# Two-layer recurrent kernel: the second layer's silu made by ScalarE itself, four units in a row, instead of from tanh and a product

## The reference

```python
x = silu(causal_conv4(xn @ W_in_x) + conv_b)      # 256 channels = 2 tiles of 128
dt, B, C = split(x_proj(x)); delta = softplus(dt_proj(dt) + dt_b)
s_t = s_(t-1) * exp(delta * A_n) + (delta * x) * B_n    # 16 states n per channel
y = (sum_n s * C_n + x * Dskip) * silu(xn @ W_in_z);  s_out = y @ W_out
h_e = silu(xn @ Wg_e) * (xn @ Wu_e)                # 8 experts, 512 hidden each
f = sum_e cw_e * (h_e @ Wd_e)                      # every expert, weighted
```

## Time and profile before

| | |
|---|---|
| median of 3 runs | 913.11 us (912.3 to 918.16) |
| the profiled execution's own time | 914.93 us |
| its span, first to last instruction | 913.1 us |
| PE busy | 805.6 us (88%) |
| DVE busy | 682.9 us (75%) |
| POOL busy | 490.3 us (54%) |
| ACT busy | 420.7 us (46%) |
| mean granted TensorE clock | 0.971 |

### The profile page before, as it was taken

The page is one execution under the profiler, slowest core; times in us unless marked ns, Lnnn a source line. Parts: engine busy times, 40 slices in busy tenths (PEclk is TensorE's granted clock), DMA queues, the critical chain, the costliest instruction groups (busy, mean ns, idle before and its releaser), DMA issues.

```text
span 913.1 us, 10705 instructions
## 1 busy us (share of the span) xinstructions
PE 805.6 (88%) x2312; PEld 383.6 (42%) x2312; DVE 682.9 (75%) x1096; ACT 420.7 (46%) x699; POOL 490.3 (54%) x388
## 2 busy tenths in 40 slices
PE   2858998999899988868998987999887999889997
PEld 1324444444444443333454343544343544344443
DVE  4389359927973845349879897789896889899995
ACT  2744554455455634555334633434542434563341
POOL 0086436634660553225756656656655656757773
PEclk9979999999999989998999999999998999999999
DMA  9265255332523553167744575756565745758771
GB/s 266 57 189 136 89 169 150 104 106 83 161 54 106 150 169 88 31 162 193 186 146 125 131 186 143 187 128 154 143 154 131 178 132 141 176 138 212 189 186 35
DMA packets 85851, 129.28 MB, mean 142 GB/s; under 512 B 7368, under 2 KB 28560, under 8 KB 85808
## 3 DMA queue, kind: packets, MB, share of 16 engines
q1 hardware_dynamic: 85808, 128.85, 53.7%
HBM read 125.35 MB, written 3.47 MB: 141 GB/s over the span
## 4 chain that ended last, share of the span: by engine, by line
PE 30%; DVE 16%; issue 11%; ACT 4%; DMA 3%; POOL 1%; DVEq 1%; SPq 1%; ACTq 0%; POOLq 0%
DVE state L619 6%; PE bank L1496 6%; PE bank L1504 5%; DVE bank L612 3%; PE bank L1359 3%; PE bank L1397 3%; DMA CB<-crow 3%; PE bank L1384 2%; PE bank L1386 2%; PE bank L1444 2%; PE bank L1385 2%; DVE gg L739 2%; PE bank L1314 1%; DVE hid L747 1%; ACT sg L1225 1%
## 5 line engine op out<-in xcount | busy, mean ns | idle before, releaser
L619 DVE TENSOR_TENSOR_SCAN state<-decay,bank 128x512 f32<-128x512 f32 x192 | 232.9, 1213 | 17.5 <-issue 9.1
L1384 PE MATMUL bank<-XH,wh 128*128 128x512 f32 x256 | 176.3, 689 | 25.5 <-DVE gg L739 11.1
L1496 PE MATMUL bank<-xw,wu 128*128 128x512 f32 x256 | 141.9, 637 | 36.5 <-DVE hid L747 36.2
L1179 ACT ACTIVATE decay<-delta,negA 128x510 f32<-128x510 f32 x192 | 135.7, 715 | 42.0 <-DVE state L619 41.7
L1186 ACT ACTIVATE hid<-bank,early 128x512 f32<-128x512 f32 x128 | 87.5, 685 | 142.0 <-PE bank L1444 132.2
L612 DVE TENSOR_TENSOR bank<-bank,CB 128x512 f32<-128x512 f32 x192 | 133.2, 694 | 20.6 <-DMA CB<-crow 11.5
L1444 PE MATMUL bank<-hid,wd 128*128 128x512 f32 x256 | 147.5, 659 | 0.0
L902 POOL TENSOR_TENSOR product<-state,CB 128x512 f32<-128x512 f32 x64 | 81.7, 1276 | 99.9 <-DVE state L619 99.9
L1504 PE MATMUL bank<-hid,wd 128*128 128x512 f32 x256 | 132.4, 600 | 0.0
L1225 ACT ACTIVATE sg<-bank 128x512 f32<-128x512 f32 x128 | 75.7, 592 | 99.9 <-PE bank L1386 99.9
L898 POOL TENSOR_TENSOR product<-state,CB 128x512 f32<-128x512 f32 x64 | 81.6, 1276 | 74.4 <-DVE state L619 44.4
(11 more groups left out here) (167 smaller groups left out, 922.6 us busy)
## 6 DMA issues: line engine op xcount, KB each, us to landing
CB<-crow SPq DMA_DIRECT2D x256, 256.0 KB, 5.0
CB<-crow SPq DMA_DIRECT2D x64, 512.0 KB, 4.8
cwb<-cwrow SPq DMA_DIRECT2D x32, 256.0 KB, 5.7
wu<-W_dram SPq DMA_DIRECT2D x8, 256.0 KB, 5.3
wd<-W_dram SPq DMA_DIRECT2D x8, 256.0 KB, 5.9
wu<-Wu_dram SPq DMA_DIRECT2D x8, 256.0 KB, 3.6
xw<-Wg_dram SPq DMA_DIRECT2D x8, 256.0 KB, 4.6
wd<-Wd_dram SPq DMA_DIRECT2D x8, 256.0 KB, 5.0
```

The costliest lines, as they stand in the source:

```text
L619: v.tensor_tensor_scan(state[:, c % RING, :], decay[:, c % RING, :], drive, 0.0, ALU.mult, ALU.add).then_inc(state_ready.sem, 1)
L1179: a.activation(by_batch(decay[:, c % RING, :])[:, :, 1:], by_batch(delta[:, m, :])[:, :, 1:], ACT.Exp, scale=negA[:, c:c + 1]).then_inc(de ...
L1384: t.matmul(dst, wh[:, e, ws], XH[:, :], start=True, stop=False)
L1496: t.matmul(bank[UP_BANK][:, :], wu[:, e, 128 * f:128 * f + 128], xw[:, e % 2, :], start=True, stop=True).then_inc(up_ps.sem, 1)
```

## The change

Silu becomes one activation of ACT, for the experts' gates, for `xs` and for `sz`. What DVE did for it (L739, L701, L712) is gone, and so is `half_gate`. ACT now takes four units in a row in every fourth slot, then the decays of four or five chunks. The silu results and the decays get six places each (`PLACE`) in place of two and four. PE makes four gates in two slots, and none in the other two. The head's steps get other slots; `hand_over1`, `low1`, `form_delta` and the first two decays move from slot 0 into slots 29 to 31 of the pair before. In layer 1 only buffers and one wait (`sp_c_ready` for `sp_u_ready`) differ.

```diff
-HEAD1 = {6: "stat1", 7: "var1", 9: "xn", 11: "xnT", 12: "xi0", 13: "logits", 14: "lmax", 15: "lexp",
-         16: "xs0 z0 tz0", 17: "sz0 xi1", 19: "xs1", 20: "row0", 21: "z1 tz1 soft1", 22: "sz1",
-         24: "dt0 soft2", 25: "row1 rest0 soft3", 26: "dt1 less0", 27: "cwT rest1", 28: "less1 ln", 29: "xr"}
+HEAD1 = {6: "stat1", 7: "var1", 9: "xn", 11: "xnT", 12: "logits", 13: "lmax", 14: "xi0 lexp",
+         16: "xs0 z0 sz0", 17: "row0", 18: "xi1 soft1", 20: "xs1 z1 sz1", 21: "row1 soft2", 22: "dt0 soft3",
+         23: "rest0", 25: "dt1 less0 rest1", 26: "cwT less1", 29: "ln hand xr", 30: "low del0", 31: "dec0"}
...
+SCAN1 = [at + 1 for at in CHUNKS1]
+DECAYS1 = [[c for c in range(2, C1) if FT * e + 3 <= SCAN1[c] <= FT * e + 6] for e in range(E)]
+PLACE = [k % SIX for k in range(UNITS - FT)] + [0, 1, 4, 5]
...
+def freed(k, pair):
+    earlier = [n for n in range(k) if PLACE[n] == PLACE[k]]
+    if earlier:
+        return max(earlier) + 1
+    if isinstance(pair, int) and pair == 0:
+        return 0
+    return max(n for n in range(UNITS) if PLACE[n] == PLACE[k]) + 1 - UNITS
...
     # DVE
-            def finish_gate(i, u):
-                dve.wait_ge(tanh_ready.sem, tanh_ready.at1(i, u + 1))
-                dve.wait_ge(hid_ready.sem, hid_ready.at1(i, u - 1))
-                v.scalar_tensor_tensor(out=gg[:, u % 2, :], in0=sg[:, u % 2, :], scalar=1.0, in1=bank[HID_BANK + u % HIDS][:, :],
-                                       op0=ALU.add, op1=ALU.mult).then_inc(gg_ready.sem, 1)
...
-                v.tensor_tensor(hid[:, u % 2, :], gg[:, u % 2, :], bank[UP_BANK][:, :], ALU.mult).then_inc(hid_ready.sem, 1)
+                v.tensor_tensor(hid[:, u % 2, :], sg[:, PLACE[u], :], bank[UP_BANK][:, :], ALU.mult).then_inc(hid_ready.sem, 1)
...
     # ACT, head
+                if name in ("xs0", "xs1"):
+                    act.wait_ge(*use1(head_ps, j, f"xi{m}"))
+                    act.wait_ge(kept_ready.sem, kept_ready.at1(j, 0))
+                    act.wait_ge(dx_ready.sem, dx_ready.at1(j, 0 if m == 1 or first_pair(j) else -1))
+                    a.activation(xs[:, m, :], hb[:, :], ACT.Silu, bias=col1("bconv", m)).then_inc(head_read.sem, 1)
...
-                    a.activation(sz[:, m, :], hb[:, :], ACT.Tanh, scale=0.5).then_inc(tz_ready.sem, 1)
+                    a.activation(sz[:, m, :], hb[:, :], ACT.Silu).then_inc(head_read.sem, 1)
...
     # ACT, units
+            def silu(i, u):
+                act.wait_ge(hid_ps.sem, hid_ps.at1(i, u + 1))
+                act.wait_ge(hid_ready.sem, hid_ready.at1(i, freed(u, i)))
+                a.activation(sg[:, PLACE[u], :], bank[HID_BANK + u % HIDS][:, :], ACT.Silu).then_inc(silu_ready.sem, 1)
...
+                if u % FT == 0:
+                    silu(i, u)
+                    silu(i, u + 1)
+                    for name in steps_:
+                        if name in ("xs0", "xs1"):
+                            head(name, j)
+                    silu(i, u + 2)
+                    silu(i, u + 3)
+                    for name in steps_:
+                        if name in ("sz0", "sz1"):
+                            head(name, j)
+                    for c in DECAYS1[u // FT]:
+                        form_decay(i, c)
...
     # PE
-                pe.wait_ge(gg_ready.sem, gg_ready.at1(i, bank_free(u)))
+                pe.wait_ge(silu_ready.sem, silu_ready.at1(i, bank_free(u)))
...
-                if u == 0:
+                if u == 0 and first_pair(i):
                     gate1(i, 0)
-                if u + 1 < UNITS:
+                    gate1(i, 1)
+                if u % FT == 0:
+                    gate1(i, u + 2)
+                    gate1(i, u + 3)
+                if u % FT == FT - 1 and u + 1 < UNITS:
                     gate1(i, u + 1)
+                    gate1(i, u + 2)
+                if u == UNITS - 1 and head:
+                    gate1(j, 0)
+                    gate1(j, 1)
```

More of the change, by code:

```diff
@@ L319, in in1, with first_pair @@
             return lambda signal, n: signal.at1(i, n)
+        def first_pair(j):
+            return isinstance(j, int) and j == 0
         def over_e(ap):
@@ L728, in head1 @@
                     rounding(m, sp_u_ready.at1(j, m + 1))
+                if name == "low":
+                    if not first_pair(j):
+                        low1(j)
+                if name == "del0":
+                    form_delta(lambda signal, n: signal.at1(j, n), 0, J1, decay_ready.at1(j, 0 if first_pair(j) else -N))
             def low1(i):
@@ L760, in slot1 @@
                 at = in1(i)
-                if u == 0:
+                if u == 0 and late is first_late:
                     low1(i)
-                    if late is first_late:
-                        split_low(2 * E - 1)
+                    split_low(2 * E - 1)
                 if late:
@@ L773, in slot1 @@
                 if u == 0:
[L774 removed]
+                    form_dx(at, 0, 0, 0)
                     for c in now(CHUNKS1, u):
@@ L810, in _ @@
             v.memset(XNP[:, :, 0:KC - 1], 0.0).then_inc(setup_dve.sem, 1)
-            for k in range(RING):
+            for k in range(SIX):
                 v.memset(by_batch(decay[:, k, :])[:, :, 0:1], 0.0).then_inc(setup_dve.sem, 1)
@@ L1144, in head1 @@
                 if name == "ln":
-                    act.wait_ge(sp_u_ready.sem, sp_u_ready.at1(j, J1))
+                    act.wait_ge(sp_c_ready.sem, sp_c_ready.at1(j, J1))
                     a.activation(sp_l[:, :, :], sp_u[:, :, :], ACT.Ln).then_inc(sp_l_ready.sem, 1)
                     a.activation(warm[:, :], ones[:, :], ACT.Exp)
+                if name == "hand" and not first_pair(j):
+                    hand_over1(j)
+                if name == "dec0":
+                    for c in range(2):
+                        form_decay(j, c)
                 if name in ("dt0", "dt1"):
@@ L1219, in late0 @@
                     last.then_inc(tg_ready.sem, 1)
[L1221 removed]
+            def silu(i, u):
                 act.wait_ge(hid_ps.sem, hid_ps.at1(i, u + 1))
[L1224 to L1225 removed]
+                act.wait_ge(hid_ready.sem, hid_ready.at1(i, freed(u, i)))
+                a.activation(sg[:, PLACE[u], :], bank[HID_BANK + u % HIDS][:, :], ACT.Silu).then_inc(silu_ready.sem, 1)
             def slot1(i, u, head=None, j=None, late=None):
[L1228 removed]
+                if u == 0 and late is first_late:
                     hand_over1(i)
[L1230 to L1241 removed]
+                    split_high(2 * E - 1)
+                if u == 0 and late:
+                    late(u)
+                steps_ = now(HEAD1, u) if head else []
+                if u % FT == 0:
[7 more added lines that the diff above has]
+                    for name in steps_:
+                        if name in ("sz0", "sz1"):
+                            head(name, j)
+                    for c in DECAYS1[u // FT]:
+                        form_decay(i, c)
                 if u > 0 and late:
@@ L1245, in slot1 @@
                     keep(i)
-                if head:
-                    for name in now(HEAD1, u):
+                for name in steps_:
+                    if name not in ("xs0", "xs1", "sz0", "sz1"):
                         head(name, j)
```

91 lines of the change are left out of this document (29 added, 62 removed).

## The result

The changed kernel takes 940.97 us (938.98 to 946.61, 4 runs) against 914.62 (912.3 to 918.16, 4 runs) for the kernel before on the same chip: ratio 1.0286, 95% interval 1.0245 to 1.0327. It is slower by 2.9%, where 1.3% faster was predicted, and it lies outside the range. The profiled execution has a span of 938.9 us against 913.1, and a mean granted clock of 0.939 against 0.971.

The account below looks back on a forecast made before the run. DVE bounded plain slots, PE 0.05 us behind and next. Per pair, PE's 107.9 plus five terms (4.6, 5, 4.5, 3, 1.7) made 126.7 against 130.9; three pairs save 12.6, giving 901 us against 913.1, range 884 to 922.

Parts of the forecast that it names:

- the part on what is removed: DVE's work per full pair falls to about 89 us, below PE's 108; at most 23 us per pair gained.
- PE's floor: PE's unchanged work in a full pair of layer 2: 107.9 of 130.9 us at full clock.
- Term 1: At layer 2's loop jumps: PE idle and slower matmuls, 4.6 us per pair.
- Term 3: ACT in order: PE waits for silu behind head steps, 3.0 us at slot 11; 4.5 us per pair (0 to 9).
- Term 4: DMA queue: row1's send delays loads of CB for DVE's slot 24, 3 us per pair (0 to 4).
- Term 5: Waits of 3 us lower the clock: one stretch at the lower level, 1.7 us per pair (0 to 5).
- The range: Whole kernel: forecast's own 892 to 910 us, said to come from its terms' bounds; stated range 884 to 922.
- Layer 1's last pair: Carries the first head: four more switches, half shown in PE, 2.6 us, against 2.47 of waits for sz: nothing.
- The last pair: Layer 2, slots 6 to 31: four slots take 11.6 us on PE, 11.6 before on DVE: nothing gained.
- The drain: At ACT's table loads: the page adds about 1380 ns to 1283; the prediction saw none in the trace.
- The rivals: Whole kernel: waits hide, 873 (0.14); no switch, 889 (0.06); gain given back, 913 (0.25); slower, 927 (0.13).
- Rival E: PE waits for ACT's switch and silu at seven of eight gate groups, 13.3 us per pair: 927 us, chance 0.13.

Follow-up runs that it names:

- e1: The changed kernel with DVE's rest1 moved from slot 25 to 27 and POOL's less1 from 26 to 28: 916.65 us, ratio 1.0015 to the kernel before.
- e4: The kernel before with only rest1 moved from slot 27 to 26, beside dt1: 931.93 us, ratio 1.0168.
- e7: e5 with layer 2's three pairs written out in place of the loop on DVE, POOL, ACT and PE: 894.62 us, ratio 0.9751.
- e9: The kernel before with layer 2's three pairs written out, nothing else: 902.48 us, ratio 0.9858.
- e8: e5 with tanh in place of silu in layer 2, so no table switches there (the output differs): 903.36 us, ratio 0.9853.
- e6: e5 with a timetable of its own for the head in layer 1's last pair: 907.57 us, ratio 0.9904.
- e5: The changed kernel with rest1 in slot 27, less1 in 28 and xnT in slot 10: 912.01 us, ratio 0.9944 to the kernel before.
- e3: The changed kernel with tanh in place of silu in layer 2, so no table switches there (the output differs): 927.65 us, ratio 1.0118.
- e2: The changed kernel with the transposes of xn and ACT's copy of them in slot 10, not 11: 927.14 us, ratio 1.0131.

## Why the prediction was wrong

The sign was lost in the part on what is removed, at "DVE's work falls to about 89 us per pair, well below PE's 108, so PE is next, and this gain can't be taken whole". The 89 is right (88.6), the conclusion isn't. It treats DVE as a sum of busy times. An engine that runs in order also stands where it is told to stand, and the diff gave it a new place: rest1 in the slot of dt1. I went through ACT's order step by step and not through DVE's, because DVE was the engine being relieved. The prediction says of the step that is moved nothing at all. Undoing that one move takes the time from 940.97 to 916.65, 24 of the 26 us lost (e1), and making it in the old kernel costs 16 (e4). DVE stood 5.13 us for it where the sum of a pair has nothing.

By the prediction's own steps:
- PE's floor of 107.9: not refuted. The shortest pair of all runs is 120.6 (e7).
- Term 1, the jumps, 4.6 per pair: with the pairs written out, 4.5 in the old kernel (13.5 / 3) and 5.8 in the new (17.4 / 3). Good for the old; the second stop of DVE, 3.06, and PE's 7.33 for 5.45 are what was short.
- Term 3, ACT in order: at slot 11 the mechanism and the size of the wait were right, 2.73 against 3.0. Its price was not: 14 us for three pairs when taken away alone, 4.6 per pair, and 5 to 7 in all once rest1's wait was gone. All of PE's waits for a silu in layer 2 are 10.9 us, 3.6 per full pair where the term has 4.5.
- Term 4, the queue: 22.0 us of waits for CB in layer 2 against 6.8 before, 15.2 over four pairs, where I had 3 in each of three. The send, holds the queue as it did. Taking it out of the way gave 4.0 us in one kernel and none in the next, so most of these waits weren't on the path, or followed from others.
- Term 5, the lower clock: the mechanism was named and mis-sized. With the jumps and both misplaced steps gone PE is busy 336.0 us in the three pairs at 0.99 (e7), in the changed kernel 355.1 at 0.93 on the same work: 6.4 per pair, where terms 1 and 5 together have 1.6 + 1.7 = 3.3. In the old kernel the same difference is 2.7 per pair (348.8 against 340.6 in e9). I had waits of 3 us in mind; PE stands 4.05 for rest1 and 7.33 at the jump.
- The range: it was to come "from the bounds of its terms", and doesn't. With every term at its lowest a pair is 107.9 + 4.6 + 2 = 114.5, at its highest 107.9 + 4.6 + 8 + 9 + 4 + 5 = 138.5, which gives 864 to 936 us and not 892 to 910 (the stated range, 884 to 922, was then taken from the rivals' chances). The measured pair, 136.8, lies within those bounds; the measured time, 941, lies outside even them, by layer 1's last pair.
- Layer 1's last pair, "nothing": it lost 11.8. The switches of that head cost 5.3 there (e8), where I had set half of them against a saving of 2.47. PE waits 5.4 for the silu of xs at the two z, where the old kernel had only the 2.47 for DVE's sz; a timetable that parts them brings PE's first gate 4.8 earlier (e6). The two overlap, since without switches these waits are 2.6 us, so together they explain 5 to 10 of the 11.8, and the rest stays open. The delta product, which the change moved into DVE's slot 30, stands 5.52 us for the logarithm of ACT's slot 29, and the prediction never asks what slot 30 costs; but e6 shows that this wait cost nothing.
- The last pair, "nothing": it gained 2.8. The forecast compared plain slots, which are alike; the gain lies in the slots in which DVE had a further product (4.36 and 3.50 us before), and at the end.
- The drain that the Trainium skill, "ScalarE: Activation LUTs", section "What ACT_TABLE_LOAD costs", adds to a load: none in this trace either. The load began 0.02 us behind the copy (739.87 to 739.89), and the silu 0.01 behind the load (741.17 to 741.18). The prediction was right to go by the row.

The rivals did no better. Rival E, the slower side, came out nearest in time (927) with the wrong engine: ACT's switches hold PE for a few us, not 13 per pair (e8: 1.7 per full pair in e5's timetable, e3: 3.4 in the changed one). The chance of 0.12 for slower came from that mechanism only.

With both misplaced steps mended the pair is 127.5 where 126.7 was forecast. The near hit is luck in part, since slot 11's term is gone from it and others were low. And the time is only 0.6% below the old kernel's (e5), not 1.3%, because layer 1's last pair keeps its loss (XH at 410.5 for 398.9).

## What to carry to other kernels

When a change rewrites a hand-made timetable, go down each engine's column and ask of every step whether what it waits for was made in the same slot, and by how many engines: PE to ACT to DVE in one slot made DVE stand 5 us here; with DVE's step two slots later that wait was at most 1.6. Do this for the engine that gets relieved too, for its new idle time is only useful if nothing in its order blocks what PE needs next. And price a wait of PE with what follows it: here 2.7 us cost 4.6 to 5.8. Before blaming a long wait, ask what would have ended next: DVE's 5.5 us for the logarithm were replaced by as long a wait for something else.

## What the runs showed of the hardware

- DVE stopped at two instructions in a row after one jump of a loop, 3.74 and 3.06 us, waiting for nothing that the profile shows; writing four engines' loops out left 1.4 us of such stops (e7), and took 13.5 us (old kernel) and 17.4 us (new) from two jumps.
- After a PE wait of 2.73 us the granted clock went to its lower level within the next matmuls (passes 0.43 apart, not 0.23); after one of 4.05 us it was 0.57 from 664 to 668 us. Taking such a wait away shortened PE's busy time about as much as its idle time (e1: 9.8 and 10.3 us; e2: 8.3 and 9.0). With the jumps gone the clock in layer 2's three pairs was 0.99 or 1.00, in the new and in the old kernel.
- Taking the table loads out of layer 2 (63.6 us of ACT's time in three pairs) was worth 13.3 us in one timetable and 8.6 in another: a load of 1.28 us costs what the place it stands in makes of it.
